# Unread identity products on TensorE ahead of the scores of two attentions

## The reference, cut to what matters

```python
# layer 0: 32 heads of 8, rotary positions on q and k
q = (x @ Wq).reshape(b, n, 32, 8); k, v = jnp.split(ctx @ Wkv, 2, axis=-1)
q = apply_axial_rope(q, pos_map);  k = apply_axial_rope(k, ctx_pos_map)
w = jax.nn.softmax(jnp.einsum('bqhd,bkhd->bhqk', q, k) * scale, axis=-1)
attn = jnp.einsum('bhqk,bkhd->bqhd', w, v)
x = x + attn.reshape(b, n, 256) @ Wout + bout
# then 16 experts of 128 (top 2) and a shared part of 512
# layer 1: 16 heads of 16, q and k normalised per head, the last 16 of 256 keys in a softmax of their own
# then 60 experts of 176 (top 4) and a shared part of 704
```

## Time and profile before

| what | us |
|---|---|
| median of three executions (763.17 to 768.37) | 766.54 |
| the profiled execution, its own time | 768.52 |
| its span, first to last instruction | 766.6 |
| TensorE matmul busy | 646.2 (84%) |
| VectorE busy | 425.9 (56%) |
| ScalarE busy | 297.3 (39%) |
| GpSimd busy | 259.2 (34%) |
| mean granted TensorE clock | 0.898 of full |

### The profile page before, as it was taken

The page is one execution under the profiler, slowest core; times in us unless marked ns, Lnnn a source line. Parts: engine busy times, 40 slices in busy tenths (PEclk is TensorE's granted clock), DMA queues, the critical chain, the costliest instruction groups (busy, mean ns, idle before and its releaser), DMA issues. The chain is left out here.

```text
span 766.6 us, 12462 instructions
## 1 busy us (share of the span) xinstructions
PE 646.2 (84%) x4224; PEld 388.7 (51%) x4224; DVE 425.9 (56%) x1130; ACT 297.3 (39%) x552; POOL 259.2 (34%) x403
## 2 busy tenths in 40 slices
PE   1657988887799999999569999599999999999750
PEld 1542444444566666676335556365666555555330
DVE  4668788863330767967687564448982222222116
ACT  1332777785323122423036667342214232232110
POOL 5350011111135323313101333302258677777140
PEclk9895899998599999999779999759999999999875
DMA  3086122100600464553914310099001899999907
GB/s 116 1 277 197 45 64 64 45 2 1 175 0 1 127 182 151 166 179 97 240 32 126 85 45 2 12 276 245 4 12 36 236 290 276 271 269 279 266 32 274
DMA packets 82615, 99.59 MB, mean 130 GB/s; under 512 B 11610, under 2 KB 58049, under 8 KB 82547
## 3 DMA queue, kind: packets, MB, share of 16 engines
q1 hardware_dynamic: 74738, 86.53, 39.9%
q0 software_dynamic: 5600, 8.53, 4.3%
q10 hardware_dynamic: 2208, 3.67, 1.3%
HBM read 82.42 MB, written 21.63 MB: 136 GB/s over the span
## 5 line engine op out<-in xcount | busy, mean ns | idle before, releaser
L769 DVE TENSOR_REDUCE l_mx<-ps 128x2 f32<-128x512 f32 (+2 forms) x256 | 125.9, 550 | 46.7 <-PE ps L629 46.4
L857 ACT ACTIVATE l_prob<-ps 128x1024 f32<-128x1024 f32 x96 | 98.4, 1026 | 27.0 <-PE ps L659 26.8
L629 PE MATMUL ps<-l_ks,l_qs 48*128 48x256 bf16 (+1 forms) x384 | 73.1, 305 | 26.4 <-DMA l_qs<-l_q_stacks 13.2
L1392 DVE SCALAR_TENSOR_TENSOR xs<-ps,comb,xs 128x256 f32<-128x256 f32 x128 | 55.8, 482 | 59.5 <-PE ps L1052 59.4
L674 PE MATMUL ps<-l_prob,v 128*9 128x256 f32 (+1 forms) x768 | 71.4, 395 | 1.1 <-ACT l_prob L857 1.1
L2146 POOL DMA_INDIRECT y_rows<-r_sw,row x53 | 53.4, 1008 | 44.3 <-DVE r_sw L2287 33.6
L2280 DVE TENSOR_TENSOR r_hot<-r_hot,ps 128x352 f32<-128x352 f32 (+1 forms) x35 | 15.1, 432 | 95.1 <-ACT r_hot L2255 95.1
L1141 POOL TENSOR_TENSOR r_ehid<-r_erelu 128x512 f32<-128x512 f32 x32 | 35.5, 1109 | 83.6 <-ACT r_erelu L1245 83.5
L1790 POOL DMA_INDIRECT xg<-x_rows,r_empty x53 | 56.2, 1060 | 19.9 <-issue 10.5
L1052 PE MATMUL ps<-f_w,r_ehid 128*128 128x256 f32 x256 | 60.8, 381 | 0.2
L1041 PE MATMUL ps<-xT,f_w 128*128 128x512 f32 x128 | 60.0, 593 | 0.0
(11 more groups left out here) (278 smaller groups left out, 1110.4 us busy)
## 6 DMA issues: line engine op xcount, KB each, us to landing
ew<-in_L_w SPq DMA_DIRECT2D x18, 704.0 KB, 8.1
ew13b<-in_L_w SPq DMA_DIRECT2D x12, 704.0 KB, 10.9
f_w<-in_L_w SPq DMA_DIRECT2D x32, 256.0 KB, 2.7
ew<-in_L_w SPq DMA_DIRECT2D x18, 384.0 KB, 9.8
ew2b<-in_L_w SPq DMA_DIRECT2D x12, 384.0 KB, 13.9
ew13b<-in_L_w SPq DMA_DIRECT2D x12, 352.0 KB, 13.1
l_k_stacks<-part SPq DMA_DIRECT2D x8, 384.0 KB, 3.3
l_ks<-l_k_stacks SPq DMA_DIRECT2D x32, 96.0 KB, 2.2
```

Of the source, the lines that this page charges most:

```text
L629: ins = nc.tensor.matmul(ps[:, score_bank(n) + k, qt * S:(qt + 1) * S], qs[row:row + R, u % NBUF, col, qt * P:(qt + 1) * P], ks[row:row + ...
L769: ins = nc.vector.reduce_max(mx[:, u % 2, :, s, head], one[:, :, lo:hi], AX_X)
L857: nc.scalar.activation(prob[:, n % PROBS, :, :, :].rearrange("p h k q -> p (h k q)"), ps[:, 2 + 2 * (n % 2):4 + 2 * (n % 2), :].rearrange( ...
L1392: v.scalar_tensor_tensor(m.xs[:, i, :], m.ps[:, 2 + t, 0:D], m.comb[:, i, e:e + 1], m.xs[:, i, :], ALU.mult, ALU.add).then_inc(e_added, 1)
```

## The change

A helper, `keep_running`, issues products of the 128 x 128 float32 identity with itself, repeated to 256 columns, into a bank of PSUM that holds nothing at that point and that nobody reads before it is overwritten. It carries no semaphore. It is called at nine places of TensorE's list: three in `prep_l0` (30, 15 and 7 products), four in `attention` (15 or 23 at its start, 8 or 11 ahead of the transposed maxima, 5 ahead of the late splits of layer 1, 2 ahead of the product with zeros), and 6 at the end of layer 0's experts. That makes 77 for layer 0's attention and 47 for layer 1's, 124 in all. The wait for the identity's load moves up to the first of them.

```diff
--- before.py
+++ after.py
@@ -189,6 +189,12 @@
 def transposed_copy(nc, m, i, bank, dst):
     return nc.scalar.copy(dst[:, :, i * P:(i + 1) * P],
                           m.ps[:, bank, 0:D].rearrange("p (c t) -> p c t", c=KD))
+
+
+def keep_running(nc, m, bank, count):
+
+    for _ in range(count):
+        nc.tensor.matmul(m.ps[:, bank, 0:2 * P], m.ident[:], bcast(m.ident[:], 1, 2), start=True, stop=True)
 
 
 def matmul_tile(nc, out, xT, i, w, bias=None, ones=None):
@@ -295,6 +301,9 @@
         pe.wait_ge(ld_ctx, 16)
         pe.wait_ge(ld_wkv, 16)
         for i in range(NT):
+            if i == 2:
+                pe.wait_ge(ld_const, 32)
+                keep_running(nc, m, 4, 30)
             if i >= 2:
                 pe.wait_ge(v_copied, i - 1)
                 pe.wait_ge(rot_ready, i - 1)
@@ -303,7 +312,6 @@
                                        wkv[:, side * D:(side + 1) * D], start=True, stop=True)
             ins.then_inc(kv_ps, 1)
         pe.wait_ge(v_copied, NT)
-        pe.wait_ge(ld_const, 32)
         pe.wait_ge(ld_wq, 16)
         for i in range(NT + 1):
             if i == 3:
@@ -320,9 +328,12 @@
             if i >= 1:
                 t = i - 1
                 pe.wait_ge(xt_ready, t + 1)
+                if t == 2:
+                    keep_running(nc, m, 2, 15)
                 if t >= 2:
                     pe.wait_ge(rot_ready, NT + t - 1)
                 matmul_tile(nc, ps[:, 4 + t % 2, 0:D], m.xT, t, wq).then_inc(q_ps, 1)
+        keep_running(nc, m, 2, 7)
         for s in Q_SPLITS[2:4]:
             split_tensor(nc, pe, m, s, rot_done, rest_ready).then_inc(split_ps, 1)
 
@@ -710,6 +721,7 @@
                     pe.wait_ge(out_used, i)
                 matmul_tile(nc, ps[:, out_bank(i) + 1, 0:D], m.xT, i, ow).then_inc(out_ps, 1)
 
+            keep_running(nc, m, 2, 15 if lay is L0 else 23)
             for n in range(AHEAD * UP):
                 if lay is L0 and n == 2:
                     pe.wait_ge(m.rest_ready, len(SPLITS))
@@ -722,14 +734,17 @@
                 if n == UP:
                     if late is not None:
                         pe.wait_ge(late.cent, 2)
+                    keep_running(nc, m, 6, 8 if lay is L0 else 11)
                     transposed_maxima(0)
                 if late is not None and n == UP:
                     pe.wait_ge(negT_ready, 1)
+                    keep_running(nc, m, 6, 5)
                     for k in range(2):
                         late.tensor_split(pe, k)
             if late is not None:
                 pe.wait_ge(late.rest_ready, 2)
             pe.wait_ge(zero_row_set, 1)
+            keep_running(nc, m, 6, 2)
             nc.tensor.matmul(ps[:, 6, :], m.ones_row[:], zero_row, start=True, stop=True)
             pe.wait_ge(ones_ld, 16 * RT * NBUF)
             for n in range(PAIRS + TURN_LAG + 1):
@@ -1102,6 +1117,7 @@
                 routed_outputs(n)
                 keys(n)
                 queries(n)
+            keep_running(nc, m, 0, 6)
 
         @block.gpsimd
         def _(pool):
```

## The result

The changed kernel takes 776.95 us (median of 6 runs, 773.18 to 778.67), the kernel before 764.26 in the same series (6 runs, 760.42 to 768.37): 1.42% slower, the ratio 1.0142 with a 95% interval of 1.0107 to 1.0176. The forecast was 772.0 with 763 to 778, and it gave most of its chance (0.61) to "within 1%", which did not come; "slower by more" had 0.27. The profiled execution after took 773.18 us (span 771.3), that of before 768.52 (span 766.6). The first is the shortest of its set and the second longer than all six of its own, so these two traces differ by 4.7 us where the medians differ by 12.7. Places in the traces are compared first; this comes back at the end.

A forecast was written before the change was run, and what follows sets the result against it. The chain of waits starts behind the barrier to layer 1's router, so delays in both attentions were carried to the end. Layer 0's 3.9 plus layer 1's 1.6 gave +5.5 us, on 766.54 predicting 772.0; own range 768 to 776, stated 763 to 778.

The forecast's parts named there:

- price: Cost of one helper product on TensorE, issued as two records: 0.4325 us at full clock, 0.87 at half.
- A: Layer 0's preparation, 30 products: key products of tile 2 start 4.4 us later, the last tile 2.6 later.
- B: Layer 0's preparation, 15 products: query product of tile 2 is 4.8 us late, query splits 3.0 late.
- C: End of layer 0's preparation, 7 products: the last splits are 4.1 us late.
- D: Start of layer 0's attention, 15 products: the first scores are 6.5 us late.
- E: Layer 0's first scores, 8 and 2 products: 0.3 us charged, 0.2 given back, scores of pair 8 +6.6.
- F: Layer 0, pairs 0 to 7: full clock returns 2.3 us, plus 0.4 for pair 8's scores, leaving +3.9.
- G: Start of layer 1's attention, 6 and 23 products: the first scores come 3.8 us later.
- H: Layer 1's late queries, 11 and 5 products, the last 2 hidden: scores of pair 8 come 2.8 us later.
- I: Layer 1, exponentials 0 to 4 and pair 8's scores: full clock returns 1.2 us, leaving +1.6.
- Rival 1: All groups: products cost about 0.28 us or less and fit their waits, giving 756.3 us; chance 0.12.
- rival 2: First scores: the clock falls again, F and I are lost, delays stay; +9.4 us, 775.9; chance 0.17.

The follow-up runs named there:

- e6_dense: Groups cut to fit their waits, plus products among the first scores of both layers, against the kernel before: 756.03 us against 765.37, ratio 0.988.
- e8_layer0: The counts of e6_dense in layer 0 alone, no products in layer 1, against the kernel before: 761.61 us, ratio 0.9944.
- e2_narrow: The changed kernel with its 124 products at 128 columns instead of 256, against the kernel before: 763.08 us, ratio 0.9943.
- e1_fit: The changed kernel with every group cut to its wait, 77 products instead of 124, against the kernel before: 761.84 us against 766.22, ratio 0.9939.

## Why the forecast was right in its first half and wrong in its second

What the excess does was right, step by step; what the clock does in the first scores was not. That the time still lies within 763 to 778 is in part luck: it is outside the forecast's own 768 to 776, and as differences the forecast was +5.5 us and +12.7 was measured. The kernel before had a median of 764.26 in this series, not the 766.54 to which the forecast was added, so 2.3 us of the miss don't show in the time. The steps, as times late, offset taken off, layer 1 relative to its own start:

| step | place | forecast | measured |
|---|---|---|---|
| price | one product, full clock | 0.4325 | 0.443 |
| A | key products of tile 2 | +4.4 | +5.3 |
| B | query product of tile 2; query splits | +4.8; +3.0 | +5.3; +3.6 |
| C | last splits | +4.1 | +4.5 |
| D | first scores | +6.5 | +6.8 |
| E | scores of pair 8 | +6.6 | +8.9 |
| F | exponential of pair 7 | +3.9 | +8.7 |
| G | first scores, layer 1 | +3.8 | +3.8 |
| H | scores of pair 8, layer 1 | +2.8 | +4.1 |
| I | exponential of pair 4, layer 1 | +1.6 | +4.9 |

**Right: the price and the excess (A to D, G).** The 0.9 us that A missed is the upper bound it had named, a clock that rises later: in the trace after, four records pass in the microsecond up to 14.7 and six in the one from 15. Rival 1 is out: its 0.28 us per product is not what the records show, and groups cut by 40% or halved in length gave 0.6% of gain each. The two records at 0.216 that the row of before showed were the price; the Trainium skill's ratio of streams to single products ("TensorE: Matmul & The Clock Gate", section "Back-to-back issue gap") would have made the loss a gain, and the trace had the streams already. Rival 1's sizes were nearly right, under a condition the change doesn't meet: in the five kernels with 18, 9 and 4 products in the preparation the first scores come 2.6 to 3.7 us early (each one's own start taken off), where A and B gave 3.7 and the heads' load now ends the wait.

**Wrong: the clock in the first scores (E, F, H, I), which is rival 2.** The prediction had named a dip of the clock between 58 and 81 as a sign that it is wrong, and it came. The step that failed is its "against": that the clock falls only after 3 us without a product, and that no such stretch is left. It fell at 69.6 and 79.9 although TensorE's longest wait from 65.44 to the first fall was 0.34 us, and the longest before the second 1.31; in layer 1 it fell after a wait of 1.74. So the returns F (2.7) and I (1.2) stayed away, and E cost 2.1 instead of 0.1, since eight products at a mostly halved clock hold back the scores VectorE waits for. H failed by 1.3 in the same way: its last two products, called hidden, took 1.87 us at half clock, and pair 8's scores came straight behind them and the product with zeros. Rival 2 was priced at 775.9, and the median is 776.95; but by difference it was +9.4, without the 2.0 of E and the 1.3 of H, so part of this closeness, too, comes from the two medians of before. Its deciding point was put wrongly: when pair 8's scores start, at 78.53, the clock is full, and it falls 1.3 us later.

The sizes of F and I themselves were good: 2.3 was taken for the pairs of layer 0, and the kernel with the clock held shows 13.60 - 11.28 = 2.3; for layer 1 1.2 was taken, and it shows 1.5. The kernel with the change's counts and the clock mostly held has the ratio 1.0091; the forecast, which assumed just that, was 772.0 to 766.54, or 1.007. So of the 1.4% about 0.9% is excess and 0.5% the clock, by two kernels whose intervals overlap (1.0056 to 1.0126 and 1.0107 to 1.0176) and of which the first has other products among its scores, so this split is an estimate.

**What the forecast didn't see.** It carried the difference to the end unchanged. The steps up to pair 7 and pair 4 sum to 8.7 + 4.9 = 13.6 us, and the medians differ by 12.7; but in the two traces 2.5 are gone by the last expert of layer 0 and 2.3 by layer 1's router. The windows of before show two more stretches at half clock there:

```profile
186.00:188.00 2.00, 0.45 (x3) 0.73 0.00 0
188.00:190.00 2.00, 1.97 (x6) 0.50 0.00 0
...
432.00:434.00 2.00, 2.00 (x13) 0.67 0.00 0
434.00:436.00 2.00, 2.00 (x12) 0.50 0.03 6
```

After the change the first of these falls comes only at 202 to 204 and the second not at all. From pair 4 to the router's first step pass 83.6 us before (494.56 - 410.93), 81.3 after (503.74 - 422.46), and 81.4 in e6_dense (482.97 - 401.61). No other execution of before was profiled, but each one's mean granted clock is on record. Of the 70 executions of before that ran beside the experiments, the 18 with 0.902 or less have a median of 767.1 us and the 11 with 0.915 or more one of 762.1; the profiled one had 0.898. After the change the two executions with 0.939, the profiled one among them, took 773.2 and 773.3 us, the four with 0.930 to 0.932 776.5 to 778.7. So the two traces compared here come from opposite ends of their sets, in clock as in time; that the clock makes all of this difference is not shown. The remaining 3.4 us, from the router to the last transfer of weights, stay open: between these two points pass 211.3 us before, 207.9 after and 209.9 in e6_dense, and 207.5 to 211.3 in the ten traces whose chain has both, though none of these kernels differs from another there.

## What to carry to other kernels

Work that only keeps TensorE busy must be shorter than the wait it fills: price it from a row of the same shape as the instruction is issued (a float32 product was two records), and cut it to the shortest wait you see, since the excess delays everything in order behind it. Then follow the clock into the stage that was to profit: a full clock at its start is worth little if the stage loses it after 4 us: groups that fit gave 0.6% (0.2 to 1.0), with products between the scores 1.2% (0.9 to 1.5), and those between the scores alone nothing in the median. Before you extend such a gain, look at what ends the program: here the last transfer of weights stands in every chain, and 6 us won at the router were worth nothing at the end.

## What the hardware showed unexpectedly

- The clock fell while TensorE was 0.91 occupied over the 11.5 us that include the start of the scores (10.52 of 11.5; 3.02 of the last 4), with no wait over 0.34 us behind the last group of products. In e6_dense, with products between the scores, it was occupied for 4.00, 3.87, 3.85 and 3.51 of each 4 us and kept 1.00; the same layer 0 code lost it for some 3.5 us in e8_layer0. So the held clock is not assured, and what tells the two apart was not settled.
- The Trainium skill ("TensorE: Matmul & The Clock Gate", section "What's actually happening") puts the penalty of the ramp under 1% of a typical span; it speaks of the products at a kernel's start. Here the clock fell several times, and the kernel that avoids most of the half-clock stretches in both attentions gained 1.2% (0.9 to 1.5).
- The heads' load landed 3.2 us later in one execution than in another whose preparation was equally quick (first scores at 58.66 in e2_narrow and 55.48 in e1_fit), which is as much as the whole preparation had to give.
